# Rotary partner by a neighbour exchange on VectorE instead of a second projection

## The reference

```python
rot_even = x_even * cos - x_odd * sin
rot_odd  = x_odd * cos + x_even * sin
```

## Time and profile before

| | us |
|---|---|
| median of 3 runs | 1118.36 (1117.96 to 1123.08) |
| the profiled execution | 1119.13 |
| its span, first to last instruction | 1117.3 |
| TensorE matmul busy | 952.8 (85%) |
| VectorE busy | 776.6 (70%) |
| ScalarE busy | 581.0 (52%) |
| GpSimd busy | 436.6 (39%) |

### The profile page before, as it was taken

How to read it: one execution, slowest core, us unless ns; L and a number is a source line. 1 busy time by engine, 2 the same in 40 slices (tenths; PEclk the granted TensorE clock), 3 DMA queues, 4 the chain that set the end, 5 groups by cost and what they waited for, 6 DMA issues and landing times.

```text
span 1117.3 us, 20415 instructions
## 1 busy us (share of the span) xinstructions
PE 952.8 (85%) x6981; PEld 825.7 (74%) x6981; DVE 776.6 (70%) x1538; ACT 581.0 (52%) x1112; POOL 436.6 (39%) x479
## 2 busy tenths in 40 slices
PE   2798878748987999999837888885989999999995
PEld 2577667536877999999825767665678888888885
DVE  5688787866664777777655687795686666667665
ACT  5375675745234667667546877874622232322221
POOL 1465556240663666666415444334012212212210
PEclk9989999859998999999956899996899999999999
DMA  3300750010325888888540000001000001000002
GB/s 129 110 21 1 189 144 1 1 61 1 128 82 193 237 231 233 227 221 233 119 134 1 20 20 1 1 2 43 15 15 29 28 14 28 17 26 28 14 0 76
DMA packets 44281, 85.81 MB, mean 77 GB/s; under 512 B 4161, under 2 KB 31041, under 8 KB 44097
## 3 DMA queue, kind: packets, MB, share of 16 engines
q0 software_dynamic: 14784, 46.44, 15.1%
q1 hardware_dynamic: 29440, 38.61, 11.9%
HBM read 64.25 MB, written 20.79 MB: 76 GB/s over the span
## 4 chain that ended last, share of the span: by engine, by line
PE 48%; DVE 20%; ACT 11%; issue 9%; DMA 7%; POOL 4%; DVEq 0%; ACTq 0%; POOLq 0%
PE bank L1179 31%; PE bank L1215 8%; DMA w_raw<-in_fw,w_idx 4%; DVE nmax L1034 3%; PE bank L1274 3%; DVE probT_lo L1063 2%; PE bank L1364 2%; DVE prob L1037 2%; POOL sorted_x L375 2%; ACT xn L512 2%; DMA summed<-y_sb,tile_to 2%; ACT probT_hi L654 1%; ACT o_raw L644 1%; PE bank L1343 1%; ACT w_hi L533 1%
## 5 line engine op out<-in xcount | busy, mean ns | idle before, releaser
L1179 PE MATMUL bank<-xT_hi,w_hi 128*128 128x512 f32 x352 | 139.9, 398 | 2.2 <-DVE hid L964 2.2
L581 ACT ACTIVATE act_sb<-bank 128x512 f32<-128x512 f32 x88 | 52.6, 598 | 167.8 <-PE bank L1179 167.7
L1179 PE MATMUL bank<-xT_lo,w_hi 128*128 128x512 f32 x352 | 139.3, 396 | 0.0
L1179 PE MATMUL bank<-xT_hi,w_lo 128*128 128x512 f32 x352 | 139.1, 395 | 0.0
L964 DVE TENSOR_TENSOR hid<-bank,act_sb 128x512 f32<-128x512 f32 x88 | 60.8, 691 | 107.3 <-ACT act_sb L581 107.1
L332 POOL TENSOR_TENSOR w_hi<-w_raw,zero_col 128x768 fp32r<-128x768 f32 (+1 forms) x20 | 31.9, 1595 | 262.9 <-PE bank L1215 236.8
L951 DVE SCALAR_TENSOR_TENSOR xres<-bank,gate,xres 128x256 f32<-128x256 f32 x320 | 132.6, 476 | 0.8 <-PE bank L1215 0.8
L1364 PE MATMUL bank<-ident,prob 128*128 128x128 f32 x512 | 86.2, 298 | 31.9 <-DVE probT_lo L1063 26.0
L1063 DVE TENSOR_TENSOR probT_lo<-bank,probT_hi 128x512 f16<-128x512 f32 x128 | 88.0, 687 | 32.4 <-ACT probT_hi L654 31.8
L1179 PE MATMUL bank<-xsT_hi,w_hi 128*128 128x256 f32 x368 | 106.5, 289 | 2.3 <-DVE xsT_lo L918 1.5
L1215 PE MATMUL bank<-w_hi,hid_hi 128*128 128x256 f32 x352 | 99.5, 283 | 6.2 <-DVE hid_lo L972 6.2
(11 more groups left out here) (199 smaller groups left out, 2763.5 us busy)
## 6 DMA issues: line engine op xcount, KB each, us to landing
w_raw<-in_fw SPq DMA_DIRECT2D x18, 384.0 KB, 3.0
sorted_x<-empty_row SPq DMA_DIRECT2D x2, 2967.0 KB, 21.4
xs<-sorted_x SPq DMA_DIRECT2D x23, 258.0 KB, 3.4
ctx_raw<-in_ctxT SPq DMA_DIRECT2D x8, 512.0 KB, 5.2
aw_raw<-in_aw SPq DMA_DIRECT2D x10, 256.0 KB, 3.8
summed<-empty_row SPq DMA_DIRECT2D x1, 2304.0 KB, 29.6
xres<-in_x SPq DMA_DIRECT2D x4, 512.0 KB, 5.7
xn_all<-summed SPq DMA_DIRECT2D x4, 512.0 KB, 5.9
```

What stands on the lines that cost most here:

```text
L581: nc.scalar.activation(act_sb[:, (ls * J + j) % 2, :], bank[2 * ((ls * J + j) % 2) + 1][:], ACT.Silu).then_inc(f["act"], 1)
L1179: last = nc.tensor.matmul(dst, lh, rh, start=(i == 0), stop=(i == len(pairs) - 1))
```

## The change

The partner is no longer projected. VectorE reads the one projection twice: times cosine into `qk`, times signed sine into `rope_b`. Then it waits for that second result and exchanges neighbouring partitions of `rope_b` in place with a stream shuffle (128x512). The sign of the sine belongs to the neighbour then, so GpSimd subtracts instead of adding. A unit of layer 0 is six matmuls, `bank[2*r+1]` is not used by it, and only four weights of layer 0 are loaded and split. The semaphore `s_rope` counts 12 per block in place of 8. VectorE's loop over blocks 0 to 2 is written out, in both layers.

```diff
--- before.py
+++ after.py
@@ -194,14 +194,15 @@
         NSORT = P + E0 + E0 * E0 + TILES + 1
         PAIRS = TILES // 2
 
-        NW = [6, 4]
+        NW = [4, 4]
         JT = [2, 1]
 
 
         V_W, O_W = [4, 2], [5, 3]
-        W_ORDER = [[2, 3, 0, 1, 4, 5], [1, 2, 0, 3]]
+        W_ORDER = [[2, 0, 4, 5], [1, 2, 0, 3]]
         KV_WEIGHTS = 2
-        UNIT_W = [[(2, 3), (2, 3), (0, 1), (0, 1)], [(1,), (1,), (0,), (0,)]]
+        UNIT_W = [[(2,), (2,), (0,), (0,)], [(1,), (1,), (0,), (0,)]]
+        PAIR = [r ^ 1 for r in range(32)]
         GROUPS = BLK * NG
         HALF = UNITS // 2
         STEPS = 2 * NBLK
@@ -438,9 +439,9 @@
 
                 def rotate(m, i):
 
-                    pool.wait_ge(s_rope, m * 8 + 2 * (i + 1))
+                    pool.wait_ge(s_rope, m * 12 + 3 * (i + 1))
                     dst = qk[:, i % 2, :] if i < 2 else q_full[:, i % 2, :]
-                    nc.gpsimd.tensor_tensor(dst, qk[:, i % 2, :], rope_b[:, i % 2, :], ALU.add).then_inc(a["qk"], 1)
+                    nc.gpsimd.tensor_tensor(dst, qk[:, i % 2, :], rope_b[:, i % 2, :], ALU.subtract).then_inc(a["qk"], 1)
 
                 def outputs(n, build):
 
@@ -673,9 +674,9 @@
                 if l == 0:
                     ln_act(0)
                     context_high(0)
-                    weights_high(range(4))
+                    weights_high(range(2))
                     unit_high(0, 0)
-                    weights_high(range(4, NW[0]))
+                    weights_high(range(2, NW[0]))
                     for i in range(1, 4):
                         unit_high(0, i)
                     values_high(0)
@@ -1004,10 +1005,12 @@
                         for c, dst in enumerate((qk, rope_b)):
                             nc.vector.scalar_tensor_tensor(
                                 out=dst[:, r].rearrange("p (b s) -> p b s", b=BLK),
-                                in0=bank[2 * r + c][:].rearrange("p (b s) -> p b s", b=BLK),
-                                scalar=bias_col[l][:, 4 * c + i:4 * c + i + 1],
+                                in0=bank[2 * r][:].rearrange("p (b s) -> p b s", b=BLK),
+                                scalar=bias_col[l][:, i:i + 1],
                                 in1=rope_tab[:, i // 2, c].unsqueeze(1).to_broadcast([P, BLK, S]),
                                 op0=ALU.add, op1=ALU.mult).then_inc(s_rope, 1)
+                        dve.wait_ge(s_rope, m * 12 + 3 * i + 2)
+                        nc.vector.stream_shuffle(rope_b[:, r], rope_b[:, r], PAIR).then_inc(s_rope, 1)
 
                 def unit_low(m, i):
                     if i < 2:
@@ -1088,7 +1091,7 @@
 
                 if l == 0:
                     ln_dve(0, lambda n: dve.wait_ge(s_x[n], 16))
-                    weights_low(range(4))
+                    weights_low(range(2))
                     dve.wait_ge(s_ident, 16)
                     nc.vector.tensor_reduce(half_col[:], ident[:].rearrange("p (r j d) -> p j r d", r=NG, j=2), AX.XY,
                                             ALU.add).then_inc(s_half, 1)
@@ -1097,7 +1100,7 @@
                         unit_build(0, i)
                         unit_low(0, i)
                         if i == 0:
-                            weights_low(range(4, NW[0]))
+                            weights_low(range(2, NW[0]))
                     values(0)
                     first_constants()
                 else:
@@ -1113,7 +1116,7 @@
                     values(0)
                 for g in range(NG):
                     shifted(0, g)
-                with dve.Fori(0, NBLK - 1) as n:
+                for n in range(NBLK - 1):
                     attend(n, True)
                 attend(NBLK - 1, False)
                 ln_dve(2 * l + 1, lambda n: dve.wait_ge(a["xadd"], 2 * n + 2))
@@ -1422,7 +1425,7 @@
                     ln_pe(0)
                     pe.wait_ge(LN["ln_lo"], 2 * NBLK)
                     for i in range(4):
-                        pe.wait_ge(a["aw_lo"], 4 if i >= 2 else 2)
+                        pe.wait_ge(a["aw_lo"], 2 if i >= 2 else 1)
                         unit(0, i, True)
                     pe.wait_ge(a["aw_lo"], NW[0])
                     values(0)
```

## The result

The changed kernel takes 1129.97 us, median of 7 runs (1126.46 to 1130.63); the kernel before, in the same jobs, 1120.79 (1117.04 to 1124.51). The ratio of the runs on record is 1.0076, 95% interval 1.0052 to 1.0100: slower by 0.8% (the two medians alone would give 1.0082). The profiled execution took 1130.03 us.

What follows compares the result with a forecast made beforehand. The prediction took a ring of VectorE and GpSimd to bound layer 0's boundaries, TensorE just behind. Ring +4.8, clock +5.7 and start -0.5 gave +10.0 on 1119.13, so 1129.1, or 1128.4 us against the median; range 1120 to 1136.

Steps and rivals of the forecast that it cites:

- What bounds: Layer 0's block boundaries: VectorE and GpSimd form a ring, TensorE only just behind; VectorE's waits for TensorE offer 1.40 us each.
- The chain's share for TensorE: The chain that ended last puts 48% of the span on TensorE; read alone, it says TensorE bounds the next block's build.
- Rival 1: Layer 0 boundaries: TensorE bounds, its 5.7 us per boundary come off in full, shuffle hidden; -17 for three, 1101; chance 0.08.
- The ring: VectorE and GpSimd at layer 0 boundaries: four shuffles, 3.0 us, less 1.40 covered; +1.6 per boundary, +4.8 for three.
- The wait in front of it: VectorE, ahead of each shuffle: waiting for the result it needs makes about 0.12 us, part of the 0.75 taken.
- The clock: Thinner TensorE work lets its clock fall before the value projection at layer 0 boundaries: +1.9 us each, +5.7 for three.
- 14 to all 24 matmuls at 0.09 us more each ... I take 1.9: Value projection at each boundary: slow matmuls until the full clock returns, 1.2 to 2.2 us, 1.9 taken.
- with no slack: Output transposes at 95.89 follow the value projection's 24 matmuls directly, so its delay passes on in full.
- The start: First units of layer 0: earlier unit 0 against shuffles and a possible slow value projection; -1.0 to +1.2 us, -0.5 taken.
- At nothing: Fewer loads and weight parts, GpSimd's subtraction for addition, and VectorE's written-out loop: no change in time expected.

Runs made afterwards that it cites:

- e1: Changed kernel with the shuffle left out, GpSimd subtracting the unexchanged product, so layer 0's rotary part is not computed: 1117.65 us, ratio to the kernel before 0.9995.
- e2: Kernel before with only VectorE's loop over blocks written out in both layers: 1119.00 us, ratio to the kernel before 0.9997.
- e7: Changed kernel with a second, identity shuffle ahead of the exchange in each of the 16 units: 1141.03 us, ratio to the kernel before 1.0186.
- e10: Changed kernel with unread matmuls in TensorE's holes, at the first block's unit 3 and at each boundary: 1123.87 us, ratio to the kernel before 1.0035.
- e3: Changed kernel with TensorE making each unit of layer 0 twice, the second copy unread: 1128.10 us, ratio to the kernel before 1.0075.
- e8: e5 plus unread matmuls: twelve ahead of the first block's unit 3, six ahead of each boundary's last weighed group: 1111.14 us, ratio to the kernel before 0.9921.
- e5: Changed kernel with GpSimd's rotation 1 ahead of output sum 4 and ScalarE making both k_half halves in layer 0: 1119.00 us, ratio to the kernel before 0.9965.

## Why the prediction was right

The forecast was 1128.4 us, 1120 to 1136, slower; measured 1129.97, with the profiled execution at 1130.03 for which 1129.1 had been summed.

**What bounds.** Right. The chain's share for TensorE misled and VectorE's idle time did not. Rival 1, which followed the chain, had 1.43 us of TensorE per unit coming off. e1 and e2 show that, counted from rden on, 1.48 per boundary does, 1.29 for the projections and 0.19 for the written-out loop, where 1.40 was read from the waits.

**The ring.** Predicted +1.6 per boundary; measured, from rden on, 13.67 + 0.11 against 12.01 + 0.29, +1.48, and +1.66 from the first qk. The shuffle was taken at 0.75 and is 0.75. The wait in front of it, 0.12, is 0.13, and e7 shows it as 0.15 between a shuffle with a dependent behind it and one without. The rule that the prediction weighed, of the Trainium skill, "VectorE: DVE Perf Modes", section "The DRAIN you can't avoid" (a semaphore after every operation costs nothing over one at the end), fits the independent passes here, each of which raises a semaphore and still has the next one begin 0.08 us before its end. It does not hold for this pair, in which the second instruction waits for the first; by it the ring would be 0.5 to 0.6 shorter at each boundary. The shuffle itself, at 0.62 us, runs like the other passes of this size, at 0.60. Behind the last probT_lo everything moved with it: 0.95 us to the value projection in both kernels (1.07 at the changed kernel's boundary 2), VectorE's wait for o_raw 1.10 and 1.11.

**The clock.** The mechanism was right, its size not. It fell in all three boundaries, but +1.9 for each was too much: +1.24, +1.02 and 0. The step that was mis-sized is "14 to all 24 matmuls at 0.09 us more each ... I take 1.9". At the first boundary the clock had risen between unit 3 and the value projection and fell again among its matmuls, at the third it was back before they began. Of the 24 matmuls some 16 were slow at boundary 1, 12 at boundary 2 and none at 3, not 14 to 24 at each. And the output transposes did not follow "with no slack", as the prediction read them. In the kernel before they begin 0.39 us behind the start of the last of these matmuls and just behind the end of GpSimd's last sum, for which they wait too:

```profile
95.34 0.40 POOL L458 TENSOR_TENSOR o_sb<-o_sb,rden 128x128 f32<-128x128 f32 x1
```

At the low clock they begin 0.12 us behind the last matmul. So the 24 matmuls took 1.51 and 1.29 us longer at boundaries 1 and 2, and 0.27 of each was hidden. Summed, 2.3 in place of 5.7.

**The start.** Predicted -0.5, with +1.2 as its far end; measured +0.88 up to the first boundary. Unit 0 came 3.3 us sooner as worked out (qk at 30.38, was 33.72), the value projection 1.1 sooner, and at the low clock it gave that back. In the summed prediction this made up for part of the clock term.

**The rest.** The three terms measured in the trace are 5.0 for the ring (4.8 predicted), 2.3 for the clock (5.7) and +0.9 for the start (-0.5), 8.1 in sum; with what lies between them it is 8.4 of the 10.9 us. The remaining 2.5 were not predicted and vary as much between kernels with the same code. So the closeness of 1129.1 to 1130.03 is partly luck: a clock term 3.4 too large was made up by a start 1.4 too small and by those 2.5. The two terms that carry the verdict are the ring, whose size was right, and the clock, which e10 puts at about 5 us over the whole run, 2.3 of it seen in the boundaries.

**At nothing.** The loop (e2) and GpSimd's subtraction in place of the addition (1.26 us each for k, 1.28 before) cost nothing, as said. No run takes the weights by themselves.

**Open.** Why the clock fell at boundary 1 of e3 although TensorE had the work of before, and whether e10 gains more over the changed kernel than its boundaries show: by the ratios it is 4.6 us, between the two profiled executions 3.1, of which 2.3 lie in the boundaries, and the intervals of the ratios are too wide to tell these apart.

## What to carry to other kernels

Before removing work from an engine, read how long the next engine really waits for it: that wait, not the work's duration, is what can be won, here 1.3 us of 5.7. When TensorE is relieved, its clock may follow its load down and its remaining matmuls on the path get dearer; where the holes can't be closed, matmuls that nobody reads can hold the clock. In the boundaries of e10 and e8 they did, and the ring stayed as it was (13.71 against 13.67 us, 10.12 against 10.10). Where two limits stand at the same length, test the pair: half of the unit matmuls traded for shuffles lost 0.8%, moving VectorE's waits gave nothing, and both together with the clock held gained 0.8%.

## What the runs showed that was not expected

Ninety-six matmuls more made no difference to the changed kernel that can be told (e3). Thirty that compute nothing, put into holes, took e5's ratio to before of 0.9965 (0.9933 to 0.9997) to e8's 0.9921 (0.9896 to 0.9945), about 0.4% less, though the two intervals overlap. The three boundaries of one kernel, with equal work, meet the clock differently, but two profiles of the same kernel meet it alike: 4.45, 4.23, 3.20 us and 4.46, 4.28, 3.21 for the same 24 matmuls.
